# Rows of ones in three operand stacks written by ScalarE, constant mask parts, later bias load and a new order of steps, in a decoder layer on one core

## The reference, cut to what matters

```python
# x: (4, 512, 128), ctx_1024: (4, 77, 128), mask: (4, 1, 1, 77) bool; 16 heads of 8
def attn(x):            # causal; q, k, v have biases
    scores = einsum('bntd,bnsd->bnts', q, k) / sqrt(8); masked above the diagonal with -inf
    return softmax(scores) @ v -> @ Wp + bp
def xattn(query, ctx, mask):
    scores = where(mask, -1e9, q @ k.T / sqrt(8)); return softmax(scores) @ v -> @ Wo.T
def ffn(x):             # 8 experts, the best 2 of the softmax, ties to the first
    comb = weights of the chosen two, at least 0.1 each, over their sum
    return einsum(x @ expert_W + expert_b, comb) / 2
x = x + attn(layernorm(x))
x = x + xattn(layernorm(x), ctx_1024, mask)
x = x + ffn(layernorm(x))
```

## Time and profile before

| | |
|---|---|
| median of 3 runs | 269.74 us (267.95 to 271.55) |
| profiled execution | 270.47 us |
| its span | 268.5 us |
| mean granted clock of TensorE | 0.984 of full |
| busy: PE / DVE / ACT / POOL | 94% / 77% / 61% / 51% of the span |

### The profile page before, as it was taken

How to read it: one execution, slowest core, us unless ns; L and a number is a source line. 1 busy time by engine, 2 the same in 40 slices (tenths; PEclk the granted TensorE clock), 3 DMA queues, 4 the chain that set the end, 5 groups by cost and what they waited for, 6 DMA issues and landing times.

```text
span 268.5 us, 6700 instructions
## 1 busy us (share of the span) xinstructions
PE 251.8 (94%) x2609; PEld 138.5 (52%) x2621; DVE 206.7 (77%) x406; ACT 162.9 (61%) x223; POOL 137.2 (51%) x278
## 2 busy tenths in 40 slices
PE   7998883899999999999999999999999999999994
PEld 2644431334464344454355644456564774587583
DVE  6999993686899998988899864779667963874651
ACT  4415431879888988987997999962583009501100
POOL 7998822646888776673575874633721060040000
PEclk9999998699999999999999999999999999999998
DMA  3663354300450223500310000300005000100101
GB/s 102 166 157 82 95 142 111 82 7 4 108 138 6 60 60 95 159 3 5 85 49 4 10 0 24 109 2 7 2 9 158 2 7 2 39 2 0 39 2 40
DMA packets 21635, 14.62 MB, mean 54 GB/s; under 512 B 2788, under 2 KB 21604, under 8 KB 21604
## 3 DMA queue, kind: packets, MB, share of 16 engines
q1 hardware_dynamic: 20324, 13.61, 18.8%
q10 hardware_dynamic: 1280, 0.59, 0.8%
HBM read 2.39 MB, written 1.05 MB: 13 GB/s over the span
## 4 chain that ended last, share of the span: by engine, by line
PE 74%; SPq 12%; DVE 7%; issue 2%; ACT 2%; DMA 1%; POOL 0%; ACTq 0%; POOLq 0%
PE banks L1028 13%; PE banks L1091 12%; SPq L340 9%; PE banks L1012 6%; PE banks L888 6%; PE banks L881 6%; PE banks L1050 5%; PE banks L897 5%; PE banks L971 4%; PE banks L966 4%; PE banks L1039 3%; DVE peaks L785 3%; PE banks L1077 3%; PE banks L987 2%; PE banks L1084 2%
## 5 line engine op out<-in xcount | busy, mean ns | idle before, releaser
L785 DVE TENSOR_REDUCE peaks<-banks 128x2 f32<-128x768 f32 (+3 forms) x88 | 95.1, 1121 | 16.4 <-PE banks L971 15.8
L676 ACT ACTIVATE probs<-banks 128x1024 f32<-128x1024 f32 x80 | 79.0, 1030 | 14.2 <-PE banks L1012 13.7
L573 POOL TENSOR_SCALAR_AFFINE_SELECT probs<-probs 128x512 f32<-128x512 f32 (+1 forms) x80 | 42.9, 545 | 34.5 <-ACT probs L676 34.1
L1028 PE MATMUL banks<-probs,v_s 128*32 128x256 f32 (+3 forms) x512 | 42.7, 439 | 0.0
L681 ACT ACTIVATE xprobs<-banks 77x1024 f32<-77x1024 f32 x32 | 31.0, 1020 | 7.4 <-PE banks L1039 7.3
L1012 PE MATMUL banks<-q_stack,k_stack 64*128 64x512 bf16 (+3 forms) x256 | 30.5, 309 | 3.8 <-DMA q_stack<-peaks_t 3.0
L971 PE MATMUL banks<-k_stack,q_stack 64*128 64x128 bf16 (+3 forms) x256 | 32.2, 303 | 0.0
L1091 PE MATMUL banks<-expert_w_s,scaled 128*128 128x128 f32 x256 | 31.9, 280 | 0.0
L1091 PEld LDWEIGHTS banks<-expert_w_s,scaled 128*128 128x128 f32 x256 | 29.6, 192 | 3.4 <-issue 2.9
L966 PE MATMUL banks<-causal,halves 64*128 64x128 bf16 (+3 forms) x352 | 26.1, 228 | 4.0 <-DMA k_stack<-parts_k 1.9
L855 DVE TENSOR_TENSOR scaled<-banks,normed_t 128x1024 f32<-128x1024 f32 x16 | 19.4, 1222 | 12.1 <-PE banks L1077 12.1
(11 more groups left out here) (174 smaller groups left out, 362.8 us busy)
## 6 DMA issues: line engine op xcount, KB each, us to landing
xq_stack<-parts_x SPq DMA_DIRECT2D x24, 128.0 KB, 2.4
q_stack<-parts_q SPq DMA_DIRECT2D x18, 128.0 KB, 2.4
k_stack<-parts_k SPq DMA_DIRECT2D x18, 128.0 KB, 2.4
out<-state SPq DMA_DIRECT2D x4, 256.0 KB, 2.3
state<-in_x SPq DMA_DIRECT2D x3, 256.0 KB, 3.2
q_stack<-parts_q SPq DMA_DIRECT2D x12, 64.0 KB, 2.1
expert_w_s<-in_expert_w SPq DMA_DIRECT2D x1, 512.0 KB, 4.3
xk_stack<-parts_x SPq DMA_DIRECT2D x6, 77.0 KB
```

The lines of the kernel that those rows point to most:

```text
L573: gp.affine_select(out=v, in_=v, compare_op=ALU.is_ge, fill=0.0, base=0, pattern=pattern, channel_multiplier=-1).then_inc(causal_done, 1)
L676: ac.activation(probs[:, grp % 2, u], two_banks(step), ACT.Exp, scale=SCALE).then_inc(taken_by_act, 1)
L785: ve.tensor_reduce(peaks[:, f, t, :, a:a + n], two_banks(step)[:, :, 0:n * width].rearrange("p s (h k) -> p s h k", h=n), X_AXIS, ALU.max, ...
L1028: last = te.matmul(home[32 * c:32 * c + 32, 128 * kt:S], weight.rearrange("p a b -> p (a b)"), probs[:, half, unit, c % 2, col:col + S - 1 ...
```

## The change

- `clear_stacks` has one step instead of two: VectorE clears `q_stack[1]` alone, and before it makes two columns `ones_rows` from sums over columns of the identity: for each partition the f32 whose bits are two bf16 ones, where that partition is a spare row, and 0 elsewhere. One column is of the rows of maxima, the other of the mask rows.
- `set_rows`, a new step of ScalarE (letter X, three times): writes `k_stack[1]`, `xk_stack` and `xq_stack` whole, each with one copy of a broadcast column. The clearing of `k_stack[1]` on VectorE, of the other two on GpSimd, and the six DMAs of ones into the three stacks fall away.
- The mask parts are three products of the mask with constants; before, a product and a chain of casts and subtractions.
- The four DMAs of the expert bias leave `context_keys` and become a load of their own, the last one (letter L).
- In the layer norms after the first of each batch, -mean and variance + eps go to VectorE.
- The peaks of batch 0 form two chains, e (f = 0) and J (f = 1), each in the order of u; the second waits on the two halves of the tokens of its own.
- The string ORDER is new, with 99 warm steps for 97.

Core of the diff (in the two ORDER strings the first two lines are shown):

```diff
+MASKED_PARTS = (-998244352.0, -1753088.0, -2560.0)
+TWO_ONES = 1.0 + 0x3F80 / 2.0 ** 23
...
-LOADS = ("x1", "context", "output", "x2", "x3", "later")
-CLEARS = ("causal", "v_s", "xk_stack", "xq_stack", "zeros_b", "expert_b_s", "xv_s", "rank", "chosen_rows")
+LOADS = ("x1", "context", "output", "x2", "x3", "later", "biases")
+CLEARS = ("causal", "v_s", "zeros_b", "expert_b_s", "xv_s", "rank", "chosen_rows")
+STACKS_SET = ("k_stack1", "xk_stack", "xq_stack")
...
-    c["e"] = [("peak", 0, (f, u)) for late in range(2) for f in range(2) for u in range(len(PEAKS))
-              if PEAKS[u][0] // 2 == late]
+    for f in range(2):
+        c["eJ"[f]] = [("peak", 0, (f, u)) for u in range(len(PEAKS))]
...
-    c["V"] = [("clear_stacks", 0, n) for n in range(2)]
+    c["V"] = [("clear_stacks", 0, 0)]
+    c["X"] = [("set_rows", 0, n) for n in STACKS_SET]
...
-    "aqaLLqPVPVPLPwwwwwwwwwwwwwwawwaqPaLawqbPbqacqqLKcawwwwwwwwwwwwwwwwwwwwwwwwwwwwwweeeewbwebebeebbPweKe"
-    "ewwbeKeecewweKwKKieieeKcecfewwseasLwwsfsifsfswfsfiwsfsvfsfvvsfsvsfjsvsfsvjsfsdvssvvmfsfvmcfcdsfvvmbf"
...
+    "LaqqaPVLLLwwwwwwwwwwwwwwawwaaaqPPabwwwwwwqPcbqXqXqXKawwwwwwwwwwwwwwwwwwwwwwwwwwwweebKJewwJPbbebePeww"
+    "weeKbweKecwwebKKJcJJKiwiJcJJcfwssJsJwsJsifsfvsfifsfvfsLfvsfvsfsvsfsvjvmsdsLfvjsfsvmssfvcscffvsfvfmsf"
...
+        row_sums = sb("row_sums", [128, 2, 2])
+        ones_rows = sb("ones_rows", [128, 2])
...
-        keep, neg = early[:, 0:B * S2], early[:, 512:512 + B * S2]
+        keep = early[:, 0:B * S2]
...
-        ones_stacked, mask_split, bias_wide = [sem("ones_stacked0"), sem("ones_stacked1")], sem("mask_split"), sem("bias_wide")
+        ones_stacked, mask_split, bias_wide = sem("ones_stacked"), sem("mask_split"), sem("bias_wide")
...
-        N_XK = PRODUCTS + 2 + 2 + 3
+        N_XK = PRODUCTS + 3
...
-        CLEARED_BY_DVE = ["k_stack0", "q_stack1", "k_stack1"]
-        CLEARED_BY_ACT = ["q_stack0"]
+        CLEARED_BY_DVE = ["k_stack0", "q_stack1"]
+        CLEARED_BY_ACT = ["q_stack0", *STACKS_SET]
...
-                sp.dma_start(k_stack[spare_rows(s, MAX_ROW), 0], ones_b[0:3 * PAIRS]).then_inc(ones_stacked[0], 16)
+                sp.dma_start(k_stack[spare_rows(s, MAX_ROW), 0], ones_b[0:3 * PAIRS]).then_inc(ones_stacked, 16)
...
             for step in SCHEDULE:
...
-                if kind == "load" and k in GROUPS:
+                if kind == "load" and k == "biases":
+                    wait_cleared(sp, "expert_b_s")
+                    for t in range(T):
+                        sp.dma_start(expert_b_s[E * t:E * t + E, t, :], expert_b).then_inc(biases_loaded, 16)
+                elif kind == "load" and k in GROUPS:
...
                 elif kind == "context_keys":
-                    wait_cleared(sp, "expert_b_s")
-                    for t in range(T):
-                        sp.dma_start(expert_b_s[E * t:E * t + E, t, :], expert_b).then_inc(biases_loaded, 16)
-                    wait_cleared(sp, "xq_stack")
-                    for s in range(2):
-                        sp.dma_start(xq_stack[spare_rows(s, MASK_ROW)], ones_b[0:3 * PAIRS]).then_inc(xk_stacked, 16)
-                        sp.dma_start(xk_stack[spare_rows(s, MAX_ROW)], ones_b[0:3 * PAIRS, 0:B * S2]
-                                     ).then_inc(xk_stacked, 16)
+                    wait_cleared(sp, "xk_stack")
...
                     if b == 1:
...
-                        if n == "k":
-                            for s in range(2):
-                                sp.dma_start(k_stack[spare_rows(s, MAX_ROW), b], ones_b[0:3 * PAIRS]
-                                             ).then_inc(ones_stacked[1], 16)
                     else:
...
                         if n == "q":
...
+                    else:
+                        wait_cleared(sp, "xq_stack")
...
                 elif kind == "turn_peaks":
...
                 elif kind == "ln_stats":
...
-                    gp.tensor_scalar(shift[:, n], moments[:, n, :, 0], -1.0, None, ALU.mult)
-                    link(gp.tensor_scalar(var[:, n], moments[:, n, :, 1], LN_EPS, None, ALU.add))
+                    if k == 0:
+                        gp.tensor_scalar(shift[:, n], moments[:, n, :, 0], -1.0, None, ALU.mult)
+                        link(gp.tensor_scalar(var[:, n], moments[:, n, :, 1], LN_EPS, None, ALU.add))
...
                 elif kind == "ln_norm":
...
-                elif kind == "clear" and k in ("xk_stack", "xq_stack"):
-                    gp.memset((xk_stack if k == "xk_stack" else xq_stack)[:].bitcast(F32), 0.0).then_inc(cleared, 1)
                 elif kind == "clear" and k in ("zeros_b", "expert_b_s"):
...
                 elif kind == "clear" and k == "rank":
...
                 if kind in TO_ACT:
...
-                if kind == "context_keys":
+                if kind == "set_rows":
+                    wait_cleared(act, "q_stack1")
+                    flat = {"k_stack1": k_stack[:, 1], "xk_stack": xk_stack[:], "xq_stack": xq_stack[:]}[k].rearrange(
+                        "p a q -> p (a q)").bitcast(F32)
+                    i = int(k == "xq_stack")
+                    ac.activation(flat, ones_rows[:, i:i + 1].broadcast_to([128, flat.shape[1]]), ACT.Copy, scale=1.0
+                                  ).then_inc(cleared_by_act, 1)
+                elif kind == "context_keys":
...
-                    link(ve.tensor_scalar(neg, mask_s[:], MASKED, None, ALU.mult))
-                    for i in range(2):
-                        link(ve.tensor_copy(neg_parts[:, i], neg))
-                        link(ve.tensor_tensor(neg, neg, neg_parts[:, i], ALU.subtract))
-                    ve.tensor_copy(neg_parts[:, 2], neg).then_inc(mask_split, 1)
+                    for i in range(3):
+                        last = ve.tensor_scalar(neg_parts[:, i], mask_s[:], MASKED_PARTS[i], None, ALU.mult)
+                    last.then_inc(mask_split, 1)
+                    dve.wait_ge(mask_split, 1)
...
                 elif kind == "fold_bias":
...
-                    last.then_inc(moments_ready, 1)
+                    if k == 0:
+                        last.then_inc(moments_ready, 1)
+                    else:
+                        link(last)
+                        ve.tensor_scalar(shift[:, n], moments[:, n, :, 0], -1.0, None, ALU.mult)
+                        ve.tensor_scalar(var[:, n], moments[:, n, :, 1], LN_EPS, None, ALU.add).then_inc(moments_ready, 1)
                 elif kind == "first_stats":
...
                 elif kind == "clear_stacks":
-                    ve.memset((k_stack if k else q_stack)[:, 1].bitcast(F32), 0.0).then_inc(cleared_by_dve, 1)
+                    wait_cleared(dve, "halves")
+                    for i, row in enumerate((MAX_ROW, MASK_ROW)):
+                        last = ve.tensor_reduce(row_sums[:, i], ident[:].rearrange("p (s r) -> p s r", s=2)[
+                            :, :, row:row + 17:8], X_AXIS, ALU.add)
+                    link(last)
+                    link(ve.tensor_tensor(ones_rows[:], row_sums[:, :, 0], row_sums[:, :, 1], ALU.add))
+                    link(ve.tensor_scalar(ones_rows[:], ones_rows[:], TWO_ONES, None, ALU.mult))
+                    ve.memset(q_stack[:, 1].bitcast(F32), 0.0).then_inc(cleared_by_dve, 1)
                 elif kind in FIRST_PROJECTED:
...
-                    if b == 0 and k == (0, 0):
+                    if b == 0 and u == 0:
...
-                        pe.wait_ge(ones_stacked[0], 32)
+                        pe.wait_ge(ones_stacked, 32)
...
-                    elif b == 0 and k == (0, LATE):
+                    elif b == 0 and u == LATE:
...
-                        if b == 1:
-                            pe.wait_ge(ones_stacked[1], 32)
-                        else:
+                        if b > 1:
...
```

More of the change, by code:

```diff
@@ L89 @@
 ORDER = (
[L90 to L96 removed]
+    "LaqqaPVLLLwwwwwwwwwwwwwwawwaaaqPPabwwwwwwqPcbqXqXqXKawwwwwwwwwwwwwwwwwwwwwwwwwwwweebKJewwJPbbebePeww"
+    "weeKbweKecwwebKKJcJJKiwiJcJJcfwssJsJwsJsifsfvsfifsfvfsLfvsfvsfsvsfsvjvmsdsLfvjsfsvmssfvcscffvsfvfmsf"
+    "mscdafsmfvfjsmdsmmvsgjvgsgvsgmgsgmgsgmvgvnsgsgksgswnssgkdAAsdAvAsgdvvAsgvgdsAvAsAAvnsgsgwsnAgsgvsgnb"
+    "gkvxhxnxhsknnvxshyxyxEhhvshnhxhnhxhLvshvonEshsvlhssovshhlvsBvBsByBsBcyBEshvvoBsBBdhPsEsoBhshoEhssoso"
+    "oxExxvhxyshxyxxvlvloExEsvdoEFvvpssEFoEsyssyFvsssFvvCsCFCsCvCCCvvCppEpFzCFCpFtzptppxxxtzxyzFpxyGFFpxx"
+    "xtGytptFyzztGGtwwDDDtDDGDDwDGDGtzGDzwwwwtGwxxxGxwyGxxyxxtytyHHHGHwwzHtzwHtHtztHzwHwwwwwHHtttwwwwwwww"
+    "wwwwwwHwwwwzttztztztttt"
 )
```

5 lines of the change are left out of this document (removed).

## The result

The changed kernel took 266.98 us (median of 17 runs, 266.36 to 272.66), the kernel before 269.47 us (17 runs, 267.95 to 271.55); the ratio is 0.9915, 95% interval 0.9889 to 0.9940. Faster by 0.9%, where I had forecast 2% and a range of 261 to 269.5 around 264. Its first profile is one of the last kind.

A forecast was written before the change was run, and what follows sets the result against it. SP's DMA issuing was taken to bind until 46.3 us, then PE. 270.47 - 7.0 (lead at batch 1) + 0.6 (norms) + 0.4 (warm steps) = 264.5 profiled, 263.7 on the median; forecast 264.0, range 261 to 269.5.

The forecast's parts named there:

- SP's queue: Early DMA issues before the first maxima: 7.12 us taken out, so SP ends batch 1's k at 36.3 for 43.44.
- DVE is late next, not SP: Before the first scores: SP free 1.3 us before the transposed maxima at 37.6; first scores at 40.5 instead of 46.34.
- DVE at the start: Before the maxima: DVE waits for ACT, mask work 3.4 us for 4.3, maxima from 21.6, 1.9 us later than before.
- Until batch 1: To batch 1's first exp: clock holds, 21.5 us from 41.1 to 62.6, 7.0 us ahead, bounds 4 to 8.2.
- After it: Later stages: norm steps moved to DVE add 3.6 us of its work; cost taken +0.6, bounds -0.5 to +3.6.
- given back to DVE: Rival, chance 0.22: where DVE is at 92%, PE waits for maxima and 3.6 us of norm steps come onto the path; 267.5.
- The counts of peaks, scores and values ahead of each later stage are within one or two in the two orders: Late stages: the new order itself costs nothing; only two more warm steps, 0.4 us.
- as a shift of the rest: Time gained before 46.3 us, where SP's issuing binds, moves everything after it forward.
- The prediction's own signs: Wrong if first scores fall outside 39 to 42.5, or batch 1's lead is gone at 240 us through a PE wait.
- the rivals: Given back to DVE 0.22, transfers bind 0.05, nothing left to gain 0.08, more 0.10, slower through the clock 0.05.

The follow-up runs named there:

- ones_back: Changed kernel with the six DMAs of ones issued again in their old places in SP's queue; 271.57 us, ratio 1.0061 to the kernel before.
- five_loads_late: Kernel before, with only x3 and the four expert bias loads moved behind batch 0's first turn_peaks; 265.74 us, ratio 0.9879.
- norm_on_pool: Changed kernel with -mean and variance + eps of the later norms back on GpSimd; 268.85 us, ratio 0.9980 to the kernel before.
- old_order_edits: Changed kernel with all its edits but the order of before throughout; 265.38 us, ratio 0.9858 to the kernel before.
- shortened choose: Changed kernel without batch 0's second-best expert search, six DVE operations; 266.28 us, ratio 0.9897. Same edit with the old order from batch 2 on: 265.13 us.
- the hybrids: Kernels whose ORDER joins new order and order of before at a step; at full clock, old order from batch 2 on 265.3 us, for batch 2's stretch only 268.0.
- second profile: Profile of another execution of the unmodified changed kernel; 267.6 us of span, mean clock 0.987.
- the second set: The changed kernel run again without modification, 12 runs; 267.82 us, ratio 0.9954 to the kernel before.
- mask_chain_back: Changed kernel with the mask parts made by the old chain of casts and subtractions; 268.88 us, ratio 0.9985 to the kernel before.
- new_to_b2_then_old: Changed kernel in the new order up to batch 2's first scores, then the order of before; 265.3 us at a clock of 0.997 or more.

## Why the prediction was wrong

*SP's queue* was right in the cause, which was shown from both sides (ones_back, five_loads_late). In size it was 1.9 us off: SP was done at 34.4 for 36.3. The sum took out the issues that the change removes, from a profile in which two other groups of issues took 1.7 us too long. That *DVE is late next, not SP*, was right: SP waited 1.3 us for the maxima, as forecast.

*DVE at the start* was wrong by 2.4 us: maxima at 19.2 for 21.6. ACT came to its writes a microsecond earlier (13.0 for 14.1), and the mask work took 1.5 us for 3.4, because I had taken the durations of the earlier trace rows as the price of the operations. They were lengthened by GpSimd's clears, which the change takes away or has done before (below). Of the 3 us, 0.6 went to a wait for PE. Both errors were to the good: exp 1 came 7.5 us earlier for 5.9.

*Until batch 1*: exp 21 at 63.0 for 62.6, and the clock held, as I took it. The number is right by luck. The stretch from exp 1 took 23.5 us for the 21.5 forecast, with the clock at 1.00 and DVE busy for 19.9 of 23 us, and the 1.6 us by which exp 1 was early made up for it.

*After it*, the norm steps: forecast a cost of 0.6 within -0.5 and +3.6, measured a gain of about 0.6. Wrong, by little; the rival that rested on it, that the gain is given back to DVE through 3.6 us of norm steps, is refuted by norm_on_pool and by old_order_edits.

The step that failed is the one that gave the new order nothing to pay: "The counts of peaks, scores and values ahead of each later stage are within one or two in the two orders". They are so at the first scores of each batch (22 and 20, 65 and 66, 119 and 119, 174 and 175), and not in between: ahead of batch 0's third xvalues there stand 155 before and 174 after, ahead of its choose 193 and 202, ahead of its turn_gate 207 and 216. On this chain all experts of batch 0 depend. What the runs showed in its place: DVE starts the gate 7 us later than in the order of before from batch 2 on (161.65 for 154.64), PE waits 1.47 us for the mix behind choose, and at full clock the late order costs 1.6 us (266.9 for 265.3), about as much as the shortened choose gives back.

The second step that failed is the rule that what comes before 46.3 is gained "as a shift of the rest". A lead of 4 to 5 us was passed on whole by the order of before; of the 6.6 us of this one, 1.4 to 1.7 went between 180 and 200 us even with the order of before from batch 2 on. And the lead was counted from a late execution, with two slow groups of issues and a fall of the clock at 45 us, 1.0 us above the median. Together: 269.5, the median of before, - 6.6 of lead + 1.0 + 1.5 + 1.6 is 267.0, for a measured 266.9 at full clock and medians of 266.98 and 267.82. This adds up what was measured and is no test of it.

What the hybrids show is that the order of the late steps does it, and the shortened choose that DVE's chain is the wait at 170 us. What takes the 1.4 to 1.7 us between 180 and 200 us, and which of the idle places makes the clock fall in one execution and not in the next, stays open.

The prediction's own signs pointed the right way: the first scores at 39.08 were just within its 39 to 42.5, and a lead that isn't there at 240 us, where 0.5 us of it were left in the second profile, was to mean "a wait of PE for DVE or ACT between them". Of *the rivals*, none named the order. The time 267.5 of the one given back to DVE is near the measured one for another reason.

## What to carry to other kernels

When a stage bound by one queue hands over to a stage bound by PE, time taken from the queue can be passed on to the end, and here the cheapest edit, five loads moved behind the critical transfers, gave 3.5 us by the medians. Part of such a gain can be the clock: compare runs at like clock before putting it down to the queue. Before a whole new order of steps is taken with such an edit, run the edit in the old order: by the medians the old one kept 3.5 to 4.1 us, the new one 1.7 to 2.5. In comparing two orders by counts, count what stands ahead of the longest chain of dependent steps, not only the steps that fill the most time.

## What the runs showed of the hardware

The same operation of DVE on 308 bytes of mask took 0.87 us in the earlier trace rows and 0.31 us after. In the kernel before GpSimd was clearing at that time:

```profile
14.28 1.80 POOL L515 MEMSET xq_stack<- 128x2048 f32 x1
16.02 0.69 POOL L517 MEMSET zeros_b<- 24x512 bf16 x1
```

The first ends at 16.08 and DVE's operation at 16.26; the second at 16.71 and DVE's next (0.71 long) at 16.89. In mask_chain_back, with no clear beside them, the same two take 0.31 each. The page "SBUF — State Buffer" of the Trainium skill, section "SBUF: two separate sides", says that a GpSimd operation and a DVE operation in a mode that uses both of DVE's ports take a shared pair of ports as an exclusive lock for the whole instruction, and that the other blocks. The trace agrees, for these operations of DVE with one input, each of which ended 0.18 us after the clear; no row names their mode.

The granted clock of PE fell to its lower level (1.2 GHz, 0.50 of full) in single short stretches, as at 207 to 209 us of the second profile, after PE had been busy for only 0.69 of the microsecond before:

```profile
206.00:207.00 1.00, 0.69 (x7) 0.61 (x7) 1.00 (x2) 0.00 (x0) 0.00 (x0) 0.77 0.00 0
207.00:209.00 2.00, 1.98 (x27) 1.31 (x27) 1.58 (x4) 0.00 (x0) 0.00 (x0) 0.50 0.04 8
```

A step of 0.006 to 0.007 in a run's mean clock goes with 1.1 to 1.3 us (266.9, 268.2, 269.3 in the 12 runs of the second set). Such stretches come in some executions of one program and not in others: norm_on_pool had PE idle for 1.6 of the 5 us from 170 to 175 and kept its clock at 1.00. The kernel that had only 0.3 us of idle time of PE at 165 to 180 us (new_to_b2_then_old) had a mean clock of 0.997 or more in 6 of 6.
